# Key-major cross attention on Trainium2: the values product in two runs a turn, and VectorE's row in a new order

## The chip, the cores and the metric

The kernel runs as one program on one core of a Trainium2 chip. The time is that of the device for one execution, in microseconds (us). The span is the time from the first to the last record of the profiled execution. TensorE (PE) multiplies matrices into PSUM, VectorE (DVE) and ScalarE (ACT) work on SBUF and PSUM, GpSimd (POOL) works on SBUF.

## The reference, cut to what matters

The whole model is four layers, each a cross attention and a feed-forward part, over 8 batches of 256 rows of 128 numbers. The change touches only the cross attention of the last layer. There are 16 heads of 64 numbers, and every row attends to 1601 keys and to one learned null key.

```python
scale = DH ** (-0.5)
q = _split_heads(jnp.einsum('bnd,df->bnf', x, Wq))
kv = jnp.einsum('bmc,cf->bmf', context, Wkv)
k, v = jnp.split(kv, 2, axis=-1)
...
k = jnp.concatenate((nk, k), axis=-2)
v = jnp.concatenate((nv, v), axis=-2)
q = q * scale
sim = jnp.einsum('bhid,bhjd->bhij', q, k)
attn = jax.nn.softmax(sim, axis=-1)
out = jnp.einsum('bhij,bhjd->bhid', attn, v)
out = out.transpose(0, 2, 1, 3).reshape(b, -1, INNER)
out = jnp.einsum('bnf,fd->bnd', out, Wout)
```

## The kernel before, in words

`KeyMajorAttention` handles two heads at once. 8 batches times 8 pairs of heads are 64 turns of work, and all products are in float32. Keys lie on the partitions: 13 blocks of 128 keys, and two blocks make a chunk, so that there are 7 chunks (0 to 6; chunk 6 is one block). The work of one turn is spread over three iterations `i` of one loop: in iteration `i` TensorE makes the scores of turn `i` and the keys of turn `i + 1`, softmax and values of turn `i - 1` are worked on, and the values product of turn `i - 2` is made. Each engine has its own loop with this order written out by hand, and they meet through counting semaphores.

- TensorE (`pe_run`) has four groups `g` in an iteration. In each group it makes some of the values product (`pe_meet`, L2282, heads side by side on 64 columns each, the chunks named by `MEETS[g]`), a part of the values (L2217), scores (`pe_score`, L2237, heads side by side on 64 rows each) and a part of the keys (L2207, with the queries L2210 in group 0). In group 0 it transposes the peaks of the scores (L2251) and spreads the shifts (L2258). In group 2 it adds up the exponentials over the partitions (`pe_total`, L2267) ahead of `pe_meet`. `pe_total` waits for all lowered scores, because it writes the PSUM banks from which they are lowered.
- VectorE (`dve_run`) lowers the scores of turn `i - 1` by their peak (`dve_lower`, L2428, four parts for each of the two heads: 8 parts), and raises the running maximum of turn `i` over its chunks (`dve_raise`, L2407, six of them, of which the last is half as large), then `dve_peak` (L2413). It also inverts the total (L2434) and divides the finished values product (`dve_divide`, L2442). The values product of the next turn begins only after `dve_divide` (`out_done`), because it is written over the same PSUM bank.
- ScalarE (`act_run`) copies scores from PSUM (`act_keep`, L2342), takes the exponentials (`act_exp`, L2348, four for the first head after the scores of group 0, four for the second head after those of group 1), and copies values (L2320) and keys (L2325).
- GpSimd (`pool_run`) adds up the exponentials over the chunks (L2493, L2498 and after).
- The projections use two PSUM banks in turn (`due` and `number`); each bank is written again only after it was copied (`taken`). In three turns of a batch (pairs 4, 5 and 6, batches 0 to 6, 21 turns in all) the context of the next batch is transposed as well (L2199): at the places 2, 3 and 4 of the iteration. ScalarE copies those of the places 2 and 4 (L2331), VectorE those of place 3 (L2386, `dve_take_at(dve, i, 3)`). These are called context turns below. In pair 2 of the batches 1 to 7 the output product (L2223) stands at place 3, and VectorE copies it (L2388): seven output turns. 33 of the other full turns (iterations 2 to 62) are called plain.

Of the kernel before, what the change touches and what calls it, by code (L numbers as in the profile page):

```python
# [442 lines left out]
class PairedAttention:  # L443
# [418 lines left out]
    def dve_run(self, dve, out):  # L862
        self.k.nc.vector.memset(self.k.psM[:], 0.0).then_inc(self.partial_zeroed.sem, 1)
        for g in range(-2, self.pairs + 3):
            q, odd = divmod(g, 2)
            for i in range(self.NB):
                for ahead, n in self.score_slots[i]:
                    if 0 <= g + ahead < self.pairs:
                        self.dve_maximum(dve, g + ahead, n)
                        if n == self.steps - 1:  # L870
                            self.dve_shift(dve, g + ahead)
                if i == 2 and odd == 0 and 0 <= q - 2 < self.quads:
                    self.dve_divide(dve, out, q - 2)
# [1197 lines left out]
class KeyMajorAttention:  # L2071
# [13 lines left out]
    CHUNKS = (KB + 1) // 2  # L2085
    NULL = KTAIL + 1
    KEYS = KB * P
    MEETS = [range(0, 2), range(2, 4), range(4, 6), range(6, 7)]

    def __init__(self, k, mem):  # L2090
        self.k = k
# [194 lines left out]
    def pe_run(self, pe):  # L2286
# [4 lines left out]
        for i in range(-1, T + 3):  # L2291
            scores, softmax, meets = 0 <= i < T, 0 <= i - 1 < T, 0 <= i - 2 < T
            for g in range(4):
                if meets and g == 2:
                    self.pe_total(pe, i - 2)
                if meets:
                    for s in self.MEETS[g]:
                        self.pe_meet(pe, i - 2, s)
# [145 lines left out]
    def dve_run(self, dve):  # L2444
        T = self.TURNS
        self.dve_prepare(dve)
        for n in range(0, 8, 2):
            self.dve_take(dve, ("ctx", 0, n))
        for i in range(0, T + 3):
            scores, softmax, meets = 0 <= i < T, 0 <= i - 1 < T, 0 <= i - 2 < T  # L2450
            if softmax:
                self.dve_shift(dve, i - 1)
            self.dve_take_at(dve, i, 0)
            if softmax:
                for part in range(4):
                    self.dve_lower(dve, i - 1, 0, part)
            if scores:
                self.dve_raise(dve, i, 1)
            if softmax:
                self.dve_lower(dve, i - 1, 1, 0)  # L2460
                self.dve_lower(dve, i - 1, 1, 1)
            self.dve_take_at(dve, i, 2)
            if softmax:
                self.dve_lower(dve, i - 1, 1, 2)
                self.dve_lower(dve, i - 1, 1, 3)
            if scores:
                self.dve_raise(dve, i, 2)
                self.dve_raise(dve, i, 3)
            self.dve_take_at(dve, i, 3)
            self.dve_take_at(dve, i, 4)  # L2470
            if meets:
                self.dve_invert(dve, i - 2)
            if scores:
                self.dve_raise(dve, i, 4)
                self.dve_raise(dve, i, 5)
            self.dve_take_at(dve, i, 6)
            if meets:
                self.dve_divide(dve, i - 2)
            if scores:
                self.dve_raise(dve, i, 6)  # L2480
                self.dve_peak(dve, i)
# [836 lines left out]
```

## Time and profile before

| | us |
|---|---|
| median of 3 runs | 4701.62 (4699.08 to 4716.05) |
| the profiled execution's own time | 4698.77 |
| its span | 4697.0 |
| TensorE busy in the span | 3943.0 (84%) |
| VectorE | 3038.2 (65%) |
| ScalarE | 2502.7 (53%) |
| GpSimd | 1560.3 (33%) |

A row of the timeline gives the start of a merged stretch of instructions in us from the start of the span, how long it took, the engine and line, what is written and read, the shape, and how many instructions were merged. PE is a matmul, PEld the load of its weights. A float32 matmul of this kernel has two records. The ends of matmuls are modelled and overlap the next start, so that stretches of TensorE are best measured from start to start. What stands in brackets is the idle time before and who ended it. The last cross attention runs from about 2600 to 4430 us.

### The profile page before, as it was taken

The numbers are of one execution on the slowest core, as the hardware profiler recorded it, in microseconds if no ns is written. First come the engines' busy times: TensorE is split into PE (matmuls) and PEld (weight loads), VectorE is DVE, ScalarE is ACT, GpSimd is POOL, SyncE is SP. The second block draws the span as 40 slices with busy tenths as digits, with TensorE's granted clock in tenths as the row PEclk, the third lists the DMA queues.
The fourth block names the chain that finished last, engine by engine and source line by source line (L and its number), as shares of the span: only waits on it lengthen the run. The fifth ranks groups of instructions, "written<-read, shape, count | busy, mean of one in ns | idle before, by whom it ended". The sixth has DMA issues, their size and how long they took to land. (4 is left out here: it accounts for less than half of the span.)

```text
span 4697.0 us, 74532 instructions
## 1 busy us (share of the span) xinstructions
PE 3943.0 (84%) x28274; PEld 2404.3 (51%) x28274; DVE 3038.2 (65%) x5035; ACT 2502.7 (53%) x4784; POOL 1560.3 (33%) x1285
## 2 busy tenths in 40 slices
PE   2399999899199974888877899999999999999754
PEld 2133333388133333666664566666666666666442
DVE  3399989734277746333333577777777777777757
ACT  2288888733088862333331565556665656666330
POOL 0200000000300001111100477766777776677510
PEclk6599999999589986778878899999999999999877
DMA  5222221100265400000000100000000000000001
GB/s 166 63 48 51 45 47 44 26 16 16 40 88 85 62 2 27 0 0 0 0 8 17 40 15 1 15 1 15 1 15 1 15 1 15 1 1 1 6 17 33
DMA packets 119700, 123.06 MB, mean 26 GB/s; under 512 B 21264, under 2 KB 97648, under 8 KB 118992
## 3 DMA queue, kind: packets, MB, share of 16 engines
q1 hardware_dynamic: 119240, 118.27, 11.7%
q8 instruction: 205, 3.36, 0.3%
q14 instruction: 111, 0.91, 0.1%
q10 hardware_dynamic: 144, 0.52, 0.0%
HBM read 103.02 MB, written 15.73 MB: 25 GB/s over the span
## 5 line engine op out<-in xcount | busy, mean ns | idle before, releaser
L835 DVE TENSOR_REDUCE att_peak.1<-psS 128x1 f32<-128x512 f32 (+1 forms) x1024 | 580.7, 634 | 95.8 <-PE psS L705 95.7
L2498 POOL TENSOR_TENSOR key_sums_0.1<-key_sums_0.1,prob_0.1 128x512 f32<-128x512 f32 x256 | 440.5, 1721 | 28.7 <-POOL key_sums_0.1 L2498 0.4
L2498 POOL TENSOR_TENSOR key_sums_1.1<-key_sums_1.1,prob_1.1 128x512 f32<-128x512 f32 x256 | 421.4, 1646 | 28.4
L804 ACT ACTIVATE att_probT.1<-psT 128x512 f32<-128x512 f32 (+1 forms) x682 | 368.8, 568 | 75.7 <-PE psT L734 34.3
L835 DVE TENSOR_REDUCE att_peak.2<-psS 128x1 f32<-128x512 f32 (+1 forms) x512 | 266.8, 569 | 139.1 <-PE psS L705 137.2
L2407 DVE TENSOR_TENSOR att_highest.1<-att_highest.1,prob_0.1 128x1024 f32<-128x1024 f32 (+1 forms) x160 | 273.1, 1707 | 129.0 <-ACT prob_0.1 L2342 121.6
L2407 DVE TENSOR_TENSOR att_highest.1<-att_highest.1,prob_1.1 128x1024 f32<-128x1024 f32 (+1 forms) x160 | 278.6, 1742 | 115.0 <-ACT prob_1.1 L2342 107.5
L705 PE MATMUL psS<-key_stack.1,query_stack.1 64*128 64x512 bf16 (+1 forms) x1024 | 271.1, 385 | 95.7 <-DMA key_stack.1<-key_parts 48.3
L751 PE MATMUL psM<-att_probT.1,quad_values.1 128*9 128x256 f32 (+1 forms) x3840 | 306.4, 391 | 19.5 <-issue 19.5
L2428 DVE TENSOR_TENSOR prob_0.1<-prob_0.1,psO 128x1024 f32<-128x1024 f32 (+1 forms) x256 | 244.0, 1017 | 49.0 <-PE psO L2258 49.0
L2428 DVE TENSOR_TENSOR prob_1.1<-prob_1.1,psO 128x1024 f32<-128x1024 f32 (+1 forms) x256 | 243.9, 1017 | 49.0 <-PE psO L2258 49.0
L705 PEld LDWEIGHTS psS<-key_stack.1,query_stack.1 64*128 64x128 bf16 x1024 | 78.1, 93 | 355.1 <-issue 194.4
L2493 POOL TENSOR_TENSOR key_sums_0.1<-prob_0.1 128x512 f32<-128x512 f32 x64 | 92.0, 1437 | 494.9 <-ACT prob_0.1 L2348 494.9
L1799 POOL TENSOR_TENSOR head_queries.1<-queryT.1,query_sin.1 64x256 f32<-64x256 f32 x128 | 92.4, 722 | 468.5 <-DVE queryT.1 L1867 460.9
L2342 ACT COPY prob_0.1<-psS 128x1024 f32<-128x1024 f32 (+1 forms) x224 | 203.7, 954 | 72.0 <-PE psS L2237 71.9
L2342 ACT COPY prob_1.1<-psS 128x1024 f32<-128x1024 f32 (+1 forms) x224 | 203.8, 955 | 70.6 <-PE psS L2237 70.6
L807 ACT ACTIVATE att_probT.2<-psT,att_key_bias.1 128x256 f32<-128x256 f32 (+1 forms) x554 | 224.3, 482 | 23.3 <-PE psT L734 18.7
L705 PE MATMUL psS<-key_stack.2,query_stack.2 102*128 102x512 bf16 (+1 forms) x512 | 141.8, 361 | 94.2 <-DMA key_stack.2<-mask_parts 87.4
L2217 PE MATMUL psT<-wkv.1,ctxT_0.1 128*128 128x128 f32 (+1 forms) x1664 | 214.5, 280 | 6.0 <-DVE ctxT_1.1 L2386 5.9
L2217 PE MATMUL psT<-wkv.1,ctxT_1.1 128*128 128x128 f32 (+1 forms) x1664 | 214.9, 280 | 4.5 <-DVE ctxT_0.1 L2386 4.5
L2207 PE MATMUL psM<-ctxT_0.1,wkv.1 128*128 128x512 f32 (+1 forms) x512 | 213.8, 540 | 3.4 <-ACT keyT_0.1 L2325 2.0
L734 PE MATMUL psT<-query_stack.1,key_stack.1 64*128 64x256 bf16 x1279 | 214.9, 282 | 0.5 <-ACT att_probT.1 L804 0.5
(683 smaller groups left out, 8912.3 us busy)
## 6 DMA issues: line engine op xcount, KB each, us to landing
key_stack.1<-key_parts SPq DMA_DIRECT2D x384, 58.0 KB
key_stack.2<-key_parts SPq DMA_DIRECT2D x96, 200.1 KB
ctx_rows.1<-in_ctx_dram SPq DMA_DIRECT2D x8, 1536.0 KB
key_parts<-split_parts.1 SPq DMA_DIRECT2D x8, 1200.8 KB, 5.8
ctx_keys_0.1<-in_ctx_dram SPq DMA_DIRECT2D x4, 768.0 KB
ctx_keys_1.1<-in_ctx_dram SPq DMA_DIRECT2D x4, 768.0 KB
query_stack.1<-query_parts SPq DMA_DIRECT2D x192, 16.0 KB
ctx_values_0.1<-in_ctx_dram SPq DMA_DIRECT2D x4, 768.0 KB
```

The costliest lines, as they stand in the source:

```text
L705: self.k.nc.tensor.matmul(self.score_bank[m % 3][:, 0:w], self.queries(rows, g, h, s * P, P), self.keys(rows, g, h, c0, w), start=True, st ...
L734: last = self.k.nc.tensor.matmul(self.key_bank[(m + h) % 3][0:w, n * S:(n + 1) * S], self.keys(rows, g, h, col, w), self.queries(rows, g, ...
L751: last = self.k.nc.tensor.matmul(self.partial[32 * j:32 * j + self.hd + 1, :], self.vquad[0:w, q % 2, blk, j, :], self.probT[0:w, g % self ...
L804: last = self.k.nc.scalar.activation(probs[:, blks[0]:blks[-1] + 1, :].rearrange("p b q -> p (b q)"), bank[0:w, 0:len(blks) * S], ACT.Exp)
L807: last = self.k.nc.scalar.activation(probs[:, blk, :], bank[0:w, n * S:(n + 1) * S], ACT.Exp, bias=bias)
L835: self.k.nc.vector.tensor_reduce(self.peak[:, 2 * h + s, c:c + 1], self.score_bank[m % 3][:, 0:w], AX_X, ALU.max).then_inc(self.peak_done. ...
L2207: last = nc.tensor.matmul(bank[:, 0:w], self.wkv[:, t, p * P:(p + 1) * P], self.ctxT[b % 2][:, t, n * BANK:n * BANK + w], start=(t == 0), ...
L2217: last = nc.tensor.matmul(bank[0:w, kb % 4 * P:(kb % 4 + 1) * P], self.ctxT[b % 2][:, t, kb * P:kb * P + w], self.wkv[:, t, at:at + P], st ...
L2342: nc.scalar.copy(self.prob[i % 2][:, :, at:at + w], k.psS[:, 2 * (g % 2):2 * (g % 2) + 2, 0:w]).then_inc(self.kept.sem, 1)
L2407: self.k.nc.vector.tensor_tensor(own, old, new, ALU.max).then_inc(self.raised.sem, 1)
L2428: self.k.nc.vector.tensor_tensor(own, own, by, ALU.add).then_inc(self.lowered.sem, 1)
L2498: nc.gpsimd.tensor_tensor(acc, acc, own[:, h, c * BANK:(c + 1) * BANK], ALU.add).then_inc(self.summed.sem, 1)
```

## The change

`MEETS` goes from four pieces of the values product to two: chunks 0 to 3 in group 0 and chunks 4 to 6 in group 2. In groups 1 and 3 `pe_meet` is no longer called. VectorE lowers all eight parts in one row before its first raise, and takes what stands at place 3 directly behind the first raise, ahead of the second and third. The instructions are the same ones in the same number.

```diff
-    MEETS = [range(0, 2), range(2, 4), range(4, 6), range(6, 7)]
+    MEETS = [range(0, 4), (), range(4, 7), ()]
...
             if softmax:
                 for part in range(4):
                     self.dve_lower(dve, i - 1, 0, part)
+            if softmax:
+                for part in range(4):
+                    self.dve_lower(dve, i - 1, 1, part)
+            self.dve_take_at(dve, i, 2)
             if scores:
                 self.dve_raise(dve, i, 1)
-            if softmax:
-                self.dve_lower(dve, i - 1, 1, 0)
-                self.dve_lower(dve, i - 1, 1, 1)
-            self.dve_take_at(dve, i, 2)
-            if softmax:
-                self.dve_lower(dve, i - 1, 1, 2)
-                self.dve_lower(dve, i - 1, 1, 3)
+            self.dve_take_at(dve, i, 3)
             if scores:
                 self.dve_raise(dve, i, 2)
                 self.dve_raise(dve, i, 3)
-            self.dve_take_at(dve, i, 3)
             self.dve_take_at(dve, i, 4)
```

## Rows read from the trace of the kernel before

**Rows 1.** Windows: busy us of each engine in 200 us, then TensorE's granted clock.

```profile
3600.00:3800.00 200.00, 197.75 (x1354) 130.74 (x1353) 155.20 (x133) 123.70 (x178) 143.30 (x101) 1.00 0.03 9
```

**Rows 2.** Timeline, TensorE's stretches in one plain turn.

```profile
3732.09 0.66 PE L2251 MATMUL psO<-tables.1,att_peak.3 128*128 128x128 f32 x4 [0.17 <-DVE att_peak.3 L2413]
...
3737.32 0.65 PE L2210 MATMUL psM<-XT.1,wq.2 128*128 128x256 f32 x2
...
3737.91 1.95 PE L2282 MATMUL psT<-prob_0.1,values_0.1 128*64 128x256 f32 x16
...
3739.78 2.05 PE L2217 MATMUL psT<-wkv.1,ctxT_0.1 128*128 128x128 f32 x16
...
3743.69 1.98 PE L2207 MATMUL psM<-ctxT_1.1,wkv.1 128*128 128x512 f32 x4
...
3745.61 0.65 PE L2267 MATMUL psO<-key_sums_0.1,att_ones.1 128*64 128x256 f32 x4
...
3749.90 2.00 PE L2237 MATMUL psS<-qT_0.1,keyT_0.1 64*128 64x256 f32 x16
...
3753.74 0.65 PE L2282 MATMUL psT<-prob_0.1,values_0.1 66*64 66x256 f32 x4
...
3754.32 0.65 PE L2217 MATMUL psT<-wkv.1,ctxT_0.1 128*65 128x128 f32 x4
...
3757.45 1.95 PE L2282 MATMUL psT<-prob_1.1,values_1.1 128*64 128x256 f32 x16
...
3759.59 0.66 PE L2251 MATMUL psO<-tables.1,att_peak.3 128*128 128x128 f32 x4 [0.19 <-DVE att_peak.3 L2413]
```

**Rows 3.** Timeline, TensorE in iteration 1, which has no values product.

```profile
2635.36 0.65 PE L2210 MATMUL psM<-XT.1,wq.2 128*128 128x256 f32 x2
2635.85 1.95 PE L2217 MATMUL psT<-wkv.1,ctxT_0.1 128*128 128x128 f32 x16
2637.73 0.49 PE L2237 MATMUL psS<-qT_1.1,keyT_1.1 64*128 64x256 f32 x2
```

**Rows 4.** Waits: who waited for whom, us in total, times, longest.

```profile
PE psT L2217 <- DVE ctxT_1.1 L2386: 5.9, 12, 0.8
...
PE psT L2217 <- DVE ctxT_0.1 L2386: 4.5, 9, 0.8
```

**Rows 5.** Timeline, VectorE and ScalarE in the plain turn of Rows 2.

```profile
3735.01 3.81 DVE L2428 TENSOR_TENSOR prob_1.1<-prob_1.1,psO 128x1024 f32<-128x1024 f32 x4 [1.53 <-PE psO L2258]
...
3738.40 3.25 ACT L2348 ACTIVATE prob_1.1<-prob_1.1 128x1024 f32<-128x1024 f32 x4
...
3739.88 3.81 DVE L2428 TENSOR_TENSOR prob_1.1<-prob_1.1,psO 128x1024 f32<-128x1024 f32 x4
...
3747.35 1.75 DVE L2434 RECIPROCAL att_rtotal.4<-psO 128x256 f32<-128x256 f32 x1
...
3752.12 1.83 DVE L2407 TENSOR_TENSOR att_highest.1<-att_highest.1,prob_0.1 128x1024 f32<-128x1024 f32 x1 [3.03 <-ACT prob_0.1 L2342]
...
3756.09 0.41 DVE L2442 TENSOR_TENSOR att_outT.3<-psT,att_rtotal.4 128x256 f32<-128x256 f32 x1
...
3757.88 1.65 DVE L2413 TENSOR_TENSOR att_peak.3<-att_highest.1 128x512 f32<-128x512 f32 x1
```

**Rows 6.** Instructions of lines 2407 and 2428: duration in ns, least/median/greatest, first and last start.

```profile
L2407 DVE TENSOR_TENSOR att_highest.1<-att_highest.1,prob_1.1 x160: 956/1844/2327, 2642.5 to 4404.4; 128x1024 f32<-128x1024 f32 x128, 128x512 f32<-128x512 f32 x32
L2407 DVE TENSOR_TENSOR att_highest.1<-prob_0.1 x32: 1218/1220/1226, 2619.7 to 4360.9; 128x1024 f32<-128x1024 f32 x32
...
L2428 DVE TENSOR_TENSOR prob_1.1<-prob_1.1,psO x256: 414/1216/1222, 2658.8 to 4417.6; 128x1024 f32<-128x1024 f32 x128
```

**Rows 7.** Timeline, a context turn: transposed context of place 2, the copies by ScalarE.

```profile
3628.05 0.60 PE L2199 MATMUL psM<-tables.1,ctx_rows.1 128*128 128x128 f32 x4
3628.24 0.59 ACT L2320 COPY values_1.1<-psT 128x512 f32<-128x512 f32 x1 [0.22 <-PE psT L2217]
...
3628.57 2.00 PE L2237 MATMUL psS<-qT_0.1,keyT_0.1 64*128 64x256 f32 x16
3628.73 0.59 ACT L2331 COPY ctxT_1.1<-psM 128x512 f32<-128x512 f32 x1
```

## The prediction

> **What bounds the kernel now.** I read the 40 slices of the page first, to find the stage of the change, then the windows over it, then the waits in it, and last the timeline of single turns. The windows show what sets the time of this stage: TensorE is busy for 197.75 of 200 us, at a granted clock of 1.00 (its upper level, 2.4 GHz), while VectorE has 155, GpSimd 143 and ScalarE 124 [rows 1]. So a turn takes as long as TensorE's row of it, plus the few waits of TensorE that are left. In the timeline a plain turn runs from one transpose of peaks to the next, 3732.09 to 3759.59, 27.50 us [rows 2]. I call its start W and count from there. "Busy" doesn't mean that every stretch is at its shortest: the gain of this change, if any, lies inside the busy time, in what a change of kind costs, and in two small waits.
>
> The waits. The values product of chunks 0 and 1 takes 1.87 us from start to next start (3737.91 to 3739.78 is such a piece), yet at the turn's end the transposes come 2.14 us after its start (3757.45 to 3759.59): TensorE waits about 0.26 us for VectorE's peak [rows 2]. In the context turns it waits before the third piece of values until VectorE has copied the transposed context: 10.4 us in 21 waits [rows 4].
>
> **Part 1, two pieces less.** What a piece costs beyond its matmuls is read by setting a turn with it beside one without it. With it: queries 0.59 (3737.32 to 3737.91), product 1.87, values and scores 3.91 (3739.78 to 3743.69) [rows 2]. Without it: queries 0.49 (2635.36 to 2635.85) and values 1.88 up to the scores [rows 3]. Scores take 1.92 (scores and keys together 3.84, 3749.90 to 3753.74, and keys 1.92, 3743.69 to 3745.61 [rows 2]), which leaves 1.99 for values behind a product. So values are 0.10 shorter where no product precedes them, and queries 0.10. The matmuls of the product themselves: 16 records last 1.95, 4 records last 0.65, so a pair of heads costs (1.95 - 0.65) / 6 = 0.217 us, eight pairs 1.73 [rows 2]. Joined to another run, the second piece costs 1.73 in place of 1.87. Removed as a piece of its own it gives back 0.10 + 0.14 + 0.10 = 0.34 us in group 1.
>
> In group 3 the piece is chunk 6 alone: 0.58 (3753.74 to 3754.32), of which two pairs are 0.43, so 0.15; the keys ahead of it get 0.09 shorter as the queries did; for the short values behind it (65 columns) the entry is not shown by itself: at least nothing, at most the 0.10 above, and I take 0.05. That is 0.29. Together 0.63 us a turn (0.58 to 0.68), in 61 full turns (iterations 2 to 62): 38.4 us.
>
> **Part 2, TensorE's new row.** W; group 0 up to the queries' end 5.82 - 0.09 = 5.73; values and scores 3.91 - 0.10, so keys at 9.54; total at 11.46 (keys 1.92); total, product, values were 4.29 (3745.61 to 3749.90) and get the two pairs of chunk 6, 0.43, so the scores of chunks 4 and 5 start at S = 16.18; with the next keys 3.84 - 0.09, short values at 19.93; these, the last scores and keys 3.13 - 0.05, so the product of chunks 0 to 3 starts at 23.01; it takes 1.87 + 1.73, and the transposes could start at 26.61 [rows 2]. Now every waiting point of that row, against the engine that it waits for:
> - Peaks: VectorE's peak ends 3757.88 + 1.65 - 3749.90 = 9.63 after S in the old turn [rows 2, 5]; with S = 16.18 that is 25.8, 0.8 before TensorE. The wait of 0.26 goes, in 33 plain turns: 8.6 us.
> - The product of the next turn waits for the division, which ends 3756.09 + 0.41 - 3749.90 = 6.60 after S, at 22.8; TensorE comes at 23.0. Hidden by only 0.2.
> - The total waits for the last lowering. The first row of lowering starts at W + 2.92 and ends at 6.7; the second follows directly now and takes 3.81, so it ends at 10.5 [rows 5]; TensorE comes at 11.46. Hidden by 0.9.
> - VectorE must be free at S + 2.22 = 18.4 for raise 4, as before (3752.12 - 3749.90) [rows 2, 5]. From 10.5 it has raises 1, 2, 3 and the inversion of 1.75. Raises 2 and 3 with their wait took 3747.35 - 3743.69 = 3.66; the first took 1.22 while it stood before GpSimd's sums [rows 6], and now it falls among them. A raise costs up to 2.33 there. With 2.1 for it: 10.5 + 2.1 + 3.7 + 1.75 = 18.05. Just free, 0.35 to spare.
>
> The Trainium skill has a rule that speaks against this move of the first raise: the page GPSIMD Engine Reference, section Specifications, says that GpSimd shares its SBUF interfaces with VectorE and contends with VectorE instructions that have two SBUF inputs. The trace agrees on raises, 1.22 us ahead of the sums and up to 2.33 beside them; by the rule alone the first raise would take 0.9 us more, and a turn would lose up to that if VectorE's row decided it.
>
> **Part 3, context turns.** The copy of place 3 moves before raises 2 and 3. The context is ready at about 13.1, VectorE has by then raised once (at most 12.6), copies, and TensorE needs the bank only at 15.8. The waits of 10.4 us go; from start to start they are some 0.05 longer each, 11.5 us. The price lies behind the copy: raises 2 and 3 wait for it, then end at 13.8 + 2 x 2.1 = 18.0, the inversion at 19.8, and raise 4 is due at 20.2. Hidden.
>
> But something else comes early. In group 1 TensorE reaches the keys sooner, by the product that left (1.87 + 0.19), and these keys need the bank of the context of place 2, which ScalarE copies only after its four exponentials. Those end at 3738.40 + 3.25 - 3732.09 = W + 9.56 [rows 5], then come the copy of values and that of context, 0.49 apart and 0.59 long [rows 7]: done at 10.6. TensorE is there at 9.54 + 0.52 for the transposes (3628.05 to 3628.57) less the 0.09 that values save before them = 9.97 [rows 7]. A new wait of 0.65 us, 21 times: 13.7 us lost. In the plain turn the same keys wait only for the copy of group 0, long done.
>
> Output turns: the output is made at W + 15.1 and copied at 15.6, raises 2 and 3 end at 19.8, the inversion at 21.5, raise 4 is due at 22.0. Hidden by 0.5. The ends: in iteration 63, with no keys, TensorE waits for lowering, which ends 1.1 us sooner: about 0.9 gained. The first turns and the drain behind the last are unchanged, at 0 within 1 us each.
>
> **Sum.** 38.4 + 8.6 + 11.5 + 0.9 - 13.7 = 45.7, less about 0.7 for small waits on the division in the seven turns of pair 6. 45 us. The profiled execution took 4698.77 (span 4697.0), so it would take 4653.8. The median of the runs shown lies 2.9 above the profiled one; I forecast 4655.
>
> **Rivals.**
> 1. VectorE becomes the bound. Slacks of 0.2 and 0.35 us are small, and GpSimd's sums fall differently on the raises. If raises 4 and 5 took 2.33 each in place of 3.97 for both, the division would end 0.7 later, and every turn would wait 0.5: 61 x 0.5 = 30 us, 4684. If all raises take 2.33, the peak ends at 10.5 + 5 x 2.33 + 1.75 + 1.79 (division to peak) + 1.65 = 27.4 and plain turns gain 0.1 only; then 4680 to 4690. For it: the median raise is at 1.84 and VectorE has little air. Against: raises 4 and 5 together took 3.97 in the same company. 12%.
> 2. A piece costs nothing by itself; what I read as its price would be in the neighbours anyway. Then only waits change: -8.6 - 11.5 + 13.7 = -6, 4693 to 4697, no change. Against: turns with and without the piece differ cleanly [rows 2, 3]. 5%.
> 3. Slower: the second row of lowering, now wholly in one piece ahead of the raises, is slowed as raises are, 2.1 in place of 1.13 a part. It would end at 13.7, the total would wait 2.2 us, the plain turn would be 28.8, 1.3 above before, and 33 of them give +44: 4740. It decides from the point at which lowering ends later than 11.46 + 0.9 = W + 12.4. Against: half of these parts ran beside GpSimd already, and the longest of 256 took 1.222, the median 1.216 [rows 6]. 2%.
> 4. No new wait in context turns: 14 us more gain, 4641. It is within the range, 10%.
>
> The same page of the Trainium skill bears on rival 3: lowering has one input in PSUM and one in SBUF, which its rule doesn't name as contending; the trace agrees, 1.222 us at most.
>
> **How the numbers follow.** My forecast has 71% (its own range 4647 to 4670, from 0.58 or 0.68 a turn, 3 us each way, the new wait between 0.3 and 1.0, 7 us, and up to 0.15 on the division), rival 4 has 10, rival 1 has 12, rival 2 has 5, rival 3 has 2. A measurement of this kernel tells a change from none at about 0.5%, 23.5 us: faster is below 4678. The forecast, rival 4 and a quarter of rival 1 are faster: 0.84; the rest of rival 1 and rival 2 are the same: 0.14; slower is rival 3, 0.02. The range of 8 in 10 runs from rival 4 to the middle of rival 1: 4639 to 4679.
>
> **What the profile would show.** Plain turns of 26.6 us from transpose to transpose; queries 0.49 before values; runs of 32 and 20 records on L2282; no wait of L2251 for VectorE; no wait of L2217 for L2386; 21 waits of L2207 for ScalarE's L2331, 0.65 each. It would be wrong if L2282 waits for L2442 in plain turns, if raises 1 to 3 run past W + 18.4, or if the step within a long run of the product is above 0.217.

## The result, and the profile after

| | before | after |
|---|---|---|
| median of 6 runs, us | 4702.64 (4695.24 to 4716.05) | 4668.53 (4663.09 to 4681.94) |
| ratio | | 0.9928, 95% interval 0.9908 to 0.9948 |
| span of the profiled execution, us | 4697.0 | 4670.1 |

The changed kernel is faster by 34 us (24 to 43 by the interval), that is 0.72%. The forecast was 4655, 48 us below this median of before; the range of 4639 to 4679 holds the time. The direction and the terms of the gain were right, but a quarter of the forecast gain is missing, and one of the prediction's own signs of being wrong came true: the product waits for the division in plain turns.

Windows of the changed kernel: the same stretch as in [rows 1].

```profile
3600.00:3800.00 200.00, 197.51 (x1403) 137.47 (x1400) 166.08 (x133) 118.06 (x173) 147.31 (x103) 1.00 0.03 9
```

TensorE is as busy as before, but it does 1403 records in the time in which it did 1354, and VectorE went from 155 to 166 us of 200. The timeline of one plain turn of the changed kernel, TensorE's stretches, against [rows 2] and [rows 3]:

```profile
2852.12 0.66 PE L2251 MATMUL psO<-tables.1,att_peak.3 128*128 128x128 f32 x4
...
2857.36 0.65 PE L2210 MATMUL psM<-XT.1,wq.2 128*128 128x256 f32 x2
...
2857.84 1.95 PE L2217 MATMUL psT<-wkv.1,ctxT_1.1 128*128 128x128 f32 x16
...
2859.72 2.00 PE L2237 MATMUL psS<-qT_1.1,keyT_1.1 64*128 64x256 f32 x16
...
2863.57 0.65 PE L2267 MATMUL psO<-key_sums_1.1,att_ones.1 128*64 128x256 f32 x4
2864.05 2.33 PE L2282 MATMUL psT<-prob_1.1,values_1.1 128*64 128x256 f32 x20
2866.31 2.05 PE L2217 MATMUL psT<-wkv.1,ctxT_1.1 128*128 128x128 f32 x16
2868.29 2.00 PE L2237 MATMUL psS<-qT_1.1,keyT_1.1 64*128 64x256 f32 x16
...
2875.42 3.67 PE L2282 MATMUL psT<-prob_0.1,values_0.1 128*64 128x256 f32 x32 [0.24 <-DVE att_outT.3 L2442]
...
2879.02 0.66 PE L2251 MATMUL psO<-tables.1,att_peak.3 128*128 128x128 f32 x4
```

The turn takes 26.90 us from transpose to transpose, against 27.50. Queries take 0.48 and values 1.88, as they did in the turn without a product. W is again the start of the transposes, here 2852.12. The scores of chunks 4 and 5 start at W + 16.17 (forecast: 16.18). The last transposes wait for nothing any more. But the product of 32 records now waits for VectorE's division: it starts at W + 23.30 where the forecast had 23.01.

VectorE in the same turn, against [rows 5]:

```profile
2855.04 7.54 DVE L2428 TENSOR_TENSOR prob_0.1<-prob_0.1,psO 128x1024 f32<-128x1024 f32 x8 [1.53 <-PE psO L2258]
...
2862.50 2.19 DVE L2407 TENSOR_TENSOR att_highest.1<-prob_1.1 128x1024 f32<-128x1024 f32 x1
...
2864.80 4.33 DVE L2407 TENSOR_TENSOR att_highest.1<-att_highest.1,prob_1.1 128x1024 f32<-128x1024 f32 x2
...
2869.06 1.74 DVE L2434 RECIPROCAL att_rtotal.4<-psO 128x256 f32<-128x256 f32 x1
...
2870.72 4.31 DVE L2407 TENSOR_TENSOR att_highest.1<-att_highest.1,prob_1.1 128x1024 f32<-128x1024 f32 x2
...
2874.96 0.41 DVE L2442 TENSOR_TENSOR att_outT.3<-psT,att_rtotal.4 128x256 f32<-128x256 f32 x1
...
2876.75 1.64 DVE L2413 TENSOR_TENSOR att_peak.3<-att_highest.1 128x512 f32<-128x512 f32 x1
```

The eight parts of lowering end at W + 10.46, as forecast, and none takes longer beside GpSimd. The five large raises take 2.1 to 2.2 us each. Raise 4 begins when VectorE comes free, at W + 18.60, not when its scores are there. From W + 2.92 to the end of the division at W + 23.25 VectorE has no idle time. So in plain turns one chain runs through both engines and closes: transposes, shifts, all of VectorE's row up to the division, the product of 32 records, the next transposes. That chain, and not TensorE's row alone, sets the 26.90 us, although TensorE is busy for 197.51 of 200 us.

The waits of the changed kernel's TensorE in iterations 2 to 62 (who waited for whom, us in total, times, longest), against [rows 4]:

```profile
PE psT L2282 <- DVE att_outT.3 L2442: 7.9, 32, 0.3
...
PE psM L2207 <- ACT ctxT_1.1 L2331: 6.6, 12, 0.6
...
PE psM L2207 <- ACT ctxT_0.1 L2331: 4.9, 9, 0.6
```

The 21 waits for VectorE's copy of the context are gone, and 21 new ones for ScalarE's copy stand there, as the forecast had it. The first row is the one that it had at nearly nothing: it put 0.7 us for the seven turns of pair 6. Those seven don't wait; the 33 plain turns and the seven second context turns (pair 5) do.

How to compare kernels finely: before this stage the executions differ by themselves. The transposes of iteration 2 start at 2655.86 in the profile of before and at 2659.95 after, and between 2648 and 2663 in the profiles of the experiments, and nearly all of it stands ahead of anything that an edit touches: the transposes of iteration 1 already start at 2630.13 and 2634.66. What the edits touch ahead of iteration 2 is iteration 1 itself (25.73 us before, 25.29 in the changed kernel, 24.12 with the order alone). From there to the transposes of iteration 63 every turn of one kind takes the same time within some 0.03 us (one exception stands below the table). I call this stretch of 61 turns "the 61 turns": 1725.9 us before (2655.86 to 4381.74), 1691.0 after (2659.95 to 4350.96), 34.9 less. Each value is of one execution, but each kind of turn stands in it seven or 33 times. The intervals of the ratios overlap between several of the kernels with the two pieces, so it is these turns that tell those kernels apart.

### The profile page after: what moved, and what is told of

Read it like the earlier page. It is cut to its first block and busy times, and to the rows that moved or that the text cites. A ratio compares the mean times of both kernels' runs of the same rounds, so it can differ in the third digit from the quotient of the medians.

```text
span 4670.1 us, 74527 instructions
## 1 busy us (share of the span) xinstructions
PE 3915.6 (84%) x28269; PEld 2435.1 (52%) x28274; DVE 3150.6 (67%) x5035; ACT 2479.5 (53%) x4784; POOL 1585.6 (34%) x1285
## 5 line engine op out<-in xcount | busy, mean ns | idle before, releaser
L2495 POOL TENSOR_TENSOR key_sums_0.1<-key_sums_0.1,prob_0.1 128x512 f32<-128x512 f32 x256 | 448.0, 1750 | 28.7 <-POOL key_sums_0.1 L2495 0.4
L2495 POOL TENSOR_TENSOR key_sums_1.1<-key_sums_1.1,prob_1.1 128x512 f32<-128x512 f32 x256 | 435.6, 1702 | 28.4
L2407 DVE TENSOR_TENSOR att_highest.1<-att_highest.1,prob_1.1 128x1024 f32<-128x1024 f32 (+1 forms) x160 | 309.5, 1934 | 20.2 <-ACT prob_1.1 L2342 10.1
L2407 DVE TENSOR_TENSOR att_highest.1<-att_highest.1,prob_0.1 128x1024 f32<-128x1024 f32 (+1 forms) x160 | 285.1, 1782 | 38.9 <-ACT prob_0.1 L2342 30.5
L2490 POOL TENSOR_TENSOR key_sums_0.1<-prob_0.1 128x512 f32<-128x512 f32 x64 | 82.1, 1282 | 461.7 <-ACT prob_0.1 L2348 461.7
L2207 PE MATMUL psM<-ctxT_0.1,wkv.1 128*128 128x512 f32 (+1 forms) x512 | 211.5, 535 | 10.0 <-ACT ctxT_1.1 L2331 6.6
L2207 PE MATMUL psM<-ctxT_1.1,wkv.1 128*128 128x512 f32 (+1 forms) x512 | 211.5, 536 | 4.9 <-ACT ctxT_0.1 L2331 4.9
L2237 PE MATMUL psS<-qT_0.1,keyT_0.1 64*128 64x256 f32 x1664 | 214.3, 392 | 0.7 <-ACT keyT_0.1 L2325 0.7
```

The lines of the kernel that those rows point to most:

```text
L2207: last = nc.tensor.matmul(bank[:, 0:w], self.wkv[:, t, p * P:(p + 1) * P], self.ctxT[b % 2][:, t, n * BANK:n * BANK + w], start=(t == 0), ...
L2237: last = nc.tensor.matmul(k.psS[:, 2 * (g % 2) + h, blk % 2 * S:(blk % 2 + 1) * S], self.keyT[i % 2][own, blk * P:(blk + 1) * P], self.qT[ ...
L2407: self.k.nc.vector.tensor_tensor(own, old, new, ALU.max).then_inc(self.raised.sem, 1)
L2495: nc.gpsimd.tensor_tensor(acc, acc, own[:, h, c * BANK:(c + 1) * BANK], ALU.add).then_inc(self.summed.sem, 1)
```

## The experiments

In each, the turns are measured from transpose to transpose; "context turns" are those of pairs 4, 5 and 6 in this order.

| kernel | ratio to before (95%) | 61 turns | plain turn | context turns | output turn |
|---|---|---|---|---|---|
| before | | 1725.9 | 27.50 | 29.01, 29.01, 28.11 | 30.81 |
| changed | 0.9928 (0.9908 to 0.9948) | 1691.0 | 26.91 | 28.52, 28.33, 27.70 | 30.16 |
| pieces alone | 0.9939 (0.9926 to 0.9953) | 1693.6 | 26.89 | 28.59, 28.59, 27.82 | 30.16 |
| order alone | 0.9991 (0.9978 to 1.0003) | 1723.3 | 27.73 | 28.73, 28.17, 27.75 | 30.81 |
| pieces and early copy | one run | 1689.8 | 26.89 | 28.51, 28.14, 27.80 | 30.16 |
| early division | 0.9905 (0.9886 to 0.9924) | 1679.2 | 26.59 | 28.51, 28.14, 27.70 | 30.16 |
| early copies by ScalarE | 0.9887 (0.9870 to 0.9903) | 1676.7 | 26.91 | 27.90, 27.53, 27.09 | 30.16 |
| both of these | 0.9884 (0.9867 to 0.9900) | 1666.3 | 26.59 | 27.90, 27.52, 27.09 | 30.16 |
| short sums | one run | 1679.2 | 26.59 | 28.51, 28.14, 27.70 | 30.16 |
| three pieces, early division | one run | 1733.0 | 27.73 | 29.47, 28.54, 28.53 | 30.46 |
| three pieces, late division | 0.9938 (0.9913 to 0.9962) | 1697.8 | 26.90 | 28.81, 28.44, 28.00 | 30.46 |

With three pieces and the early division two of the seven first context turns take 28.9, the others 29.47.

### The two pieces alone

```diff
-    MEETS = [range(0, 2), range(2, 4), range(4, 6), range(6, 7)]
+    MEETS = [range(0, 4), (), range(4, 7), ()]
```

Expected: 

> The product in two pieces alone, VectorE's order as before. Theory (a piece costs 0.34 and 0.29 us by itself): queries take 0.49 and values behind them 1.88 again, chunks 0 to 3 take 3.60, the wait for the peak goes. The total comes at W + 11.46 and lowering ends at 11.6, so 0.2 us of wait there; plain turns 26.8 (33 x 0.7 = 23 us less). In context turns the copy by VectorE still stands behind raises 2 and 3, and TensorE comes sooner: a wait of 0.6 on ScalarE and 0.8 to 1.1 on VectorE, these turns gain nothing. Together 20 to 28 us less than before, ratio 0.994 to 0.996. Rival (a piece costs nothing, only waits changed): plain turns 27.3 to 27.5, ratio 0.998 to 1.002.

Measured: 28.7 us less by the ratio (0.9939, just beyond the expected 20 to 28), 32.3 less in the 61 turns. Its waits:

```profile
PE psM L2207 <- ACT ctxT_1.1 L2331: 6.5, 12, 0.6
...
PE psO L2267 <- DVE prob_0.1 L2428: 5.3, 23, 0.2
...
PE psO L2267 <- DVE prob_1.1 L2428: 2.3, 10, 0.2
...
PE psT L2217 <- DVE ctxT_1.1 L2386: 1.5, 4, 0.4
...
PE psT L2217 <- DVE ctxT_0.1 L2386: 1.1, 3, 0.4
```

Plain turns are 26.89, where 26.8 was expected: the total waits 0.30 from start to start (0.2 as recorded) for the last lowering. Context turns gained 0.4, 0.4 and 0.3, where I had expected nothing. VectorE's copy of the context came sooner than I had worked out, at 15.0 us into the turn in place of 16.4 before, and only seven turns show a recorded wait for it. The rival, that a piece costs nothing, is out: with it plain turns could not be below 27.3.

### The new order alone

The diff is that of the change without its first hunk.

Expected: 

> VectorE's new order alone, the product in four pieces. Theory: the 21 waits on VectorE's copy of the context go (11.5 us less), and all raises fall among GpSimd's sums at 2.1 to 2.2 us each, so that the peak of plain turns comes up to 0.25 later than before (0 to 8 us more): 3 to 11 us less, ratio 0.9975 to 0.9995; no wait on ScalarE's copy of the context. Rival (the order is what gave the gain): 20 us less or more.

Measured: no difference that can be told (0.9991), 2.6 us less in the 61 turns. The waits on the copy are gone, and the context turns are 10.4 us shorter together; plain turns are 0.24 longer, 8 us: their transposes now wait 0.50 for the peak in place of 0.26. The order trades one against the other, near the lower end of what the theory had.

### The pieces, and only the early copy

```diff
     (against the pieces alone)
                 self.dve_lower(dve, i - 1, 1, 3)
+            self.dve_take_at(dve, i, 3)
             if scores:
                 self.dve_raise(dve, i, 2)
                 self.dve_raise(dve, i, 3)
-            self.dve_take_at(dve, i, 3)
```

Expected: 

> The two pieces with VectorE's old rows of lowering and raise 1 between them, but the copy of place 3 ahead of raise 2. Theory (of VectorE's new order only the early copy is worth anything, 2.6 us): waits on VectorE's copy go, plain turns 26.89 with the wait of 0.3 before the total, context turns 0.1 to 0.4 shorter than with the pieces alone; iterations 2 to 62 within 2 us of the changed kernel's 1691, or below it. Rival (lowering in one row is needed): 1694 or more.

Measured: 1689.8, within 2 us of the changed kernel and on the better side (the context turns are shorter than with the pieces alone by 0.08, 0.45 and 0.01, where 0.1 to 0.4 was expected). So the moved copy is what the new order brings, 3.9 us beside the pieces. Lowering in one row brings nothing: it takes away the 0.30 that the total waits for lowering, and puts the 0.31 that the product waits for the division in its place.

### The division directly behind the inversion

```diff
             if meets:
                 self.dve_invert(dve, i - 2)
+                self.dve_divide(dve, i - 2)
...
-            if meets:
-                self.dve_divide(dve, i - 2)
```

Expected: 

> The changed kernel, with the division directly behind the inversion, ahead of raise 4. Theory (the 0.31 us that plain turns wait before the product is for the division, which is late because it stands behind two raises of 2.1 us): the product waits no more, the peak comes 0.3 us before TensorE needs it, plain turns 26.6; 33 x 0.31 and 7 x 0.19, 11.5 us less than the changed kernel, and in iteration 63 the idle 4 us before the product and its half clock go, 3 us more. The profiled span is 4655, the ratio to before 0.989 to 0.991. Rival (VectorE's row as a whole is the bound): the wait only moves to the peak, plain turns stay at 26.9.

Measured: plain turns 26.59, the second context turn 28.14, and the 61 turns 11.8 us shorter than in the changed kernel. The wait for the division is gone and none for the peak came:

```profile
PE psM L2207 <- ACT ctxT_1.1 L2331: 6.5, 12, 0.5
...
PE psM L2207 <- ACT ctxT_0.1 L2331: 4.9, 9, 0.5
```

The theory holds; the rival would have left plain turns at 26.9. The span was expected at 4655 and is 4662.3. Iteration 2 of this profiled execution started 3.0 us later than in the changed kernel's. Iteration 63 is 3.3 shorter, as expected (25.83 in place of 29.16), but from its end to the end of the span it is 294.3 us in place of 290.0. Of these 4.3 us 1.5 stand in the first 16 records of the values of iteration 64: they took 3.24 us in place of 1.79, since the granted clock was 0.50 from 4369 to 4372. Where the rest lies was not followed up.

### ScalarE's copies between its exponentials

```diff
             for g in range(4):
-                self.act_take_at(act, i, 2 * g)
+                if g != 1 or not softmax:
+                    self.act_take_at(act, i, 2 * g)
...
                     for part in range(4):
+                        if g == 0 and part == 2:
+                            self.act_take_at(act, i, 2)
                         self.act_exp(act, i - 1, g, part)
```

Expected: 

> The changed kernel, with ScalarE copying what stands at place 2 (values, context) behind the second of its four exponentials of the first head, not behind the fourth. Theory (the new wait of 0.6 us before the keys of group 1 in context turns is for ScalarE's copy): those 21 waits go, 8 to 13 us less than the changed kernel, context turns 0.4 to 0.6 shorter, plain turns unchanged at 26.9. Rival (the late half of the exponentials delays kept scores, raises or GpSimd's sums): a new wait of the same size elsewhere, context turns as before or plain turns longer.

Measured: 14.3 us less than the changed kernel in the 61 turns, a little more than expected. Context turns are 0.62, 0.80 and 0.61 shorter, plain turns the same. The second context turn also lost its wait for the division. This is the cause of the 21 waits: what TensorE waits for in the changed kernel is a copy queued behind exponentials that nobody needs at once. Its timeline in a context turn of the changed kernel:

```profile
3609.47 3.26 ACT L2348 ACTIVATE prob_1.1<-prob_1.1 128x1024 f32<-128x1024 f32 x4
...
3612.62 0.58 ACT L2320 COPY values_1.1<-psT 128x512 f32<-128x512 f32 x1
...
3613.08 0.60 ACT L2331 COPY ctxT_1.1<-psM 128x512 f32<-128x512 f32 x1
...
3613.74 1.98 PE L2207 MATMUL psM<-ctxT_0.1,wkv.1 128*128 128x512 f32 x4 [0.54 <-ACT ctxT_1.1 L2331]
```

### Both together

The two diffs above.

Expected: 

> Both edits on the changed kernel: the division behind the inversion, and ScalarE's copies behind its second exponential. Theory (the two waits are independent): plain turns 26.6, context turns 27.9, 27.5 and 27.1, output turns 30.16, iterations 2 to 62 together 1666 us against 1691 in the changed kernel; ratio to before 0.984 to 0.988. Rival (once both are gone VectorE's row decides, by its 0.3 us of air): plain or context turns are 0.2 or more longer than these.

Measured: 1666.3 in the 61 turns, as added up; 4642.92 us median (4641.42 to 4649.91), ratio 0.9884, which is 0.0004 above the expected span of ratios. It has the lowest time of this study, 24.7 us below the changed kernel in the 61 turns. By the ratios it can't be told from the early copies alone (0.9887); the turns tell them apart, 10.4 us in the 61. Its windows, in the stretch of [rows 1], show no idle time of TensorE at all:

```profile
3600.00:3800.00 200.00, 200.00 (x1401) 138.03 (x1401) 170.79 (x135) 121.71 (x179) 149.35 (x103) 1.00 0.03 9
```

### Short sums on GpSimd

```diff
-            nc.gpsimd.tensor_tensor(acc, acc, own[:, h, c * BANK:(c + 1) * BANK], ALU.add)
+            nc.gpsimd.tensor_tensor(acc[:, 0:8], acc[:, 0:8], own[:, h, c * BANK:c * BANK + 8], ALU.add)
```

Expected: 

> The changed kernel, in which GpSimd's middle sums (8 of 14 per turn, L2498) work on 8 columns in place of 512, so that the totals leave out most keys. Theory (raises 1 to 5 take 2.1 us in place of 1.22 because GpSimd works beside them, and that is what makes the division late): raises that stand clear of the remaining sums take 1.22, the wait before the product goes, plain turns 26.6. Rival (raises take 2.1 because of what stands before them on VectorE, or for their own operands): they stay at 2.1 and plain turns at 26.9.

Measured: plain turns 26.59 and no wait for the division, with VectorE's order untouched. The instructions of line 2407 in this kernel (ns least/median/greatest), and below them those of lines 2407 and 2428 in the changed one:

```profile
L2407 DVE TENSOR_TENSOR att_highest.1<-att_highest.1,prob_0.1 x160: 691/1225/2129, 2623.0 to 4331.1; 128x1024 f32<-128x1024 f32 x128, 128x512 f32<-128x512 f32 x32
...
L2407 DVE TENSOR_TENSOR att_highest.1<-prob_0.1 x32: 1224/1546/1558, 2620.9 to 4319.6; 128x1024 f32<-128x1024 f32 x32
```

```profile
L2407 DVE TENSOR_TENSOR att_highest.1<-att_highest.1,prob_0.1 x160: 693/1934/2122, 2626.4 to 4347.2; 128x1024 f32<-128x1024 f32 x128, 128x512 f32<-128x512 f32 x32
...
L2407 DVE TENSOR_TENSOR att_highest.1<-prob_0.1 x32: 1226/2204/2215, 2624.3 to 4334.4; 128x1024 f32<-128x1024 f32 x32
...
L2428 DVE TENSOR_TENSOR prob_0.1<-prob_0.1,psO x256: 409/1211/1222, 2637.6 to 4361.0; 128x1024 f32<-128x1024 f32 x128
```

The median raise falls from 1.93 to 1.23 us, and raise 1 from 2.20 to 1.55. Only GpSimd's work was cut, so it is what makes the raises slow, and the slow raises are what made the division late. Lowering stays at 1.21 beside the sums, in the changed kernel too.

### Three pieces, with the early division

```diff
     (against the early division)
-    MEETS = [range(0, 4), (), range(4, 7), ()]
+    MEETS = [range(0, 4), (), range(4, 6), range(6, 7)]
```

Expected: 

> The kernel with the early division (plain turns 26.59, no waits), with chunk 6 back in group 3 as a piece of its own. Theory (a piece costs by itself): 0.29 us a turn more, plain turns 26.88: 0.15 in the product, 0.09 in the keys ahead, 0.05 in the values behind. Rival (a piece costs nothing where TensorE does not wait): 26.59.

Measured: neither. Plain turns are 27.73, longer than before the change. VectorE in one of them:

```profile
2847.01 1.74 DVE L2434 RECIPROCAL att_rtotal.4<-psO 128x256 f32<-128x256 f32 x1
...
2850.41 0.42 DVE L2442 TENSOR_TENSOR att_outT.3<-psT,att_rtotal.4 128x256 f32<-128x256 f32 x1 [1.66 <-PE psT L2282]
...
2850.75 5.32 DVE L2407 TENSOR_TENSOR att_highest.1<-att_highest.1,prob_0.1 128x1024 f32<-128x1024 f32 x3
...
2857.81 0.66 PE L2251 MATMUL psO<-tables.1,att_peak.3 128*128 128x128 f32 x4 [0.78 <-DVE att_peak.3 L2413]
```

The division needs the whole product, and chunk 6 is now made in group 3. So the division held VectorE up for 1.66 us, with raises 4 to 6 and the peak queued behind it, and TensorE then waited 0.8 for the peak. I had changed two things at once. What the run does show, set beside the next one (1697.8): with chunk 6 in group 3 the early division costs 35 us in the 61 turns, where with two pieces it gained 11.8. It pays only because the product ends in group 2, that is, because of the two pieces.

### Three pieces, with the late division

The same edit against the changed kernel.

Expected: 

> The changed kernel with chunk 6 back in group 3 as a piece of its own; the division where the changed kernel has it, so that nothing on VectorE waits for chunk 6 early. Theory (a piece costs 0.29 us by itself, and TensorE waits for the division only because it now comes early): plain turns 26.59 + 0.29 = 26.88, with no wait before the product, since TensorE comes 0.7 us later after the scores of chunks 4 and 5; context turns 0.29 longer than in the changed kernel where they had no such wait, output turns 30.45; iterations 2 to 62 about 5 to 9 us more than 1691. Rival (a piece costs nothing): plain turns 26.6, about 1681.

Measured: 1697.8, 6.7 more than the changed kernel. Turns that wait for no division grew by 0.29 to 0.30: context turns 28.52 to 28.81 and 27.70 to 28.00, output turns 30.16 to 30.46. In plain turns the piece costs what the wait had cost, 26.90:

```profile
2704.03 0.65 PE L2282 MATMUL psT<-prob_1.1,values_1.1 66*64 66x256 f32 x4
2704.61 0.65 PE L2217 MATMUL psT<-wkv.1,ctxT_0.1 128*65 128x128 f32 x4
2705.19 0.70 PE L2237 MATMUL psS<-qT_1.1,keyT_1.1 64*128 64x256 f32 x4
```

The theory's 0.29 is right, and so is that TensorE only waits for the division if it comes early. In the changed kernel the second removed piece therefore gave nothing in the 33 plain turns.

## Why the prediction was right, and where it was off

- **What bounds the kernel**: right for the kernel before, where VectorE still stood idle for 3.03 us of a plain turn [rows 5], and for output turns and most context turns. In plain turns of the changed kernel it no longer held: VectorE's row up to the division has no idle time and paces the turn, which is what rival 1 said, in a milder form. With the division moved ahead of raises 4 and 5 and the copies early, TensorE's row alone sets the time again, 200.00 of 200 us busy.
- **Part 1, the price of a piece**: right. 0.63 a turn was forecast. The plain turn without any wait is 26.59 (early division, short sums); 27.50 less its wait of 0.26 is 27.24, so it is 0.65, or 39.7 us in 61 turns where 38.4 was forecast. The 0.29 for the piece of chunk 6 has a run of its own (three pieces, late division). The rest is read from rows: queries went from 0.59 to 0.48, the values behind them from 1.99 to 1.88, two runs of 1.87 became one of 3.60. What in the change from one kind of matmul to the other costs this time (the 64 columns, the weights, the PSUM bank) no run separates. The short values behind chunk 6, taken as 0.05, went from 0.58 to 0.53. Of rival 2 nothing is left.
- **Part 2, the peak**: right, the wait is gone, 8.6 us. The margin was forecast as 0.8; the peak ended 0.63 ahead of the transposes, and 0.3 of that is there only because TensorE had waited for the division. Lowering ended where forecast, and rival 3 is out.
- **Part 2, the division**: this is the step that failed, in its size. "Hidden by only 0.2" became a wait of 0.31 in 33 plain turns and of 0.19 in 7 context turns. By the early division that is 11.8 us, where 0.7 was in the sum, and 0.15 a turn at most in the forecast's own range. The cause is the estimate for raises 1 to 3: I took 2.1 and, for raises 2 and 3, the old 3.66, and had VectorE free at W + 18.05. From start to next start they took 2.30 and 4.26, and VectorE was free only at 18.60, after raise 4 had been due at 18.40. Raises 4 and 5 then took 4.24 in place of 3.97 up to the division, which ended at W + 23.25 in place of 22.8. So rival 1 came true in part, 12 of its 30 us. The upper bound of 2.33 a raise was in the text; the value that I took was too near the old mean, although the change pushes all raises among the sums.
- **The rule on shared interfaces** from the Trainium skill (GPSIMD Engine Reference, Specifications) spoke against moving raise 1. The trace agrees: raise 1 went from 1.22 to 2.20, 0.98 more where 0.9 was worked out for it, lowering stayed at 1.21, and with short sums the median raise is back at 1.23. I should have given it a larger part in the sum.
- **Part 3, context turns**: right. The 21 waits on VectorE are gone. The new 21 waits on ScalarE were forecast at 0.65 and are 0.61 from start to start: 12.9 us where 13.7 was forecast. Rival 4 is out.
- **The forecast's own number**: the sum gives 4653.8 for the profiled execution and 2.9 more for the median, 4656.7; the 4655 that was written is 1.7 below that.
- **The ends**: wrong. Iteration 63 was to gain 0.9 and lost 3.4 (25.80 to 29.16). Timeline of the kernel before there, and timeline and windows of the changed kernel:

```profile
4404.53 1.95 PE L2282 MATMUL psT<-prob_0.1,values_0.1 128*64 128x256 f32 x16 [2.96 <-DVE att_outT.3 L2442]
4407.54 0.66 PE L2251 MATMUL psO<-tables.1,att_peak.3 128*128 128x128 f32 x4 [1.06 <-DVE att_peak.3 L2413]
```

```profile
4368.79 0.70 PE L2237 MATMUL psS<-qT_1.1,keyT_1.1 64*128 64x256 f32 x4
4373.75 6.44 PE L2282 MATMUL psT<-prob_0.1,values_0.1 128*64 128x256 f32 x32 [4.26 <-DVE att_outT.3 L2442]
4380.12 0.66 PE L2251 MATMUL psO<-tables.1,att_peak.3 128*128 128x128 f32 x4
```

```profile
4370.00:4372.00 2.00, 0.00 (x0) 0.00 (x0) 1.90 (x2) 0.13 (x1) 1.86 (x2) 1.00 0.00 0
4374.00:4378.00 4.00, 4.00 (x20) 2.17 (x20) 2.67 (x2) 0.00 (x0) 3.63 (x4) 0.50 0.00 0
```

  With no keys to make, TensorE reached the product early and stood idle for 4.3 us waiting for the division. The granted clock was still 1.00 from 4370 to 4372 and 0.50, the lower level, from 4374 to 4378. The product of 32 records took 6.37 us in place of 3.60, so 2.8 of the 3.4 us stand in it. With 3.60 the turn would have been 26.4, still 0.6 longer than before: behind the division there now stand four chunks of the product ahead of the transposes, where there were two. The prediction looked at the wait for lowering alone and left out this one. No run holds the clock up by itself; with the early division the turn took 25.83.

Added up: 39.7 + 8.6 + 11.5 - 12.9 - 11.8 = 35.1, and the 61 turns are 34.9 us shorter. With iteration 63, which is 3.4 longer, and iteration 1, which is 0.4 shorter, that is 31.9; the rest of the difference in the medians, 34, is within its interval.

## What to carry to other kernels

When TensorE is "99% busy", look at what a change from one kind of matmul to another costs, by a stretch that lacks the neighbour: here 0.29 to 0.34 us for each piece of the product set between other work, and joining them gave more (39.7 us) than the removed waits together (20.1). A share of 99% doesn't say that the engine sets the pace either: follow one turn from a point back to the same point, through every engine that stands in between. When a faster bounding engine comes sooner to all its meeting points, list each with its margin, and price the other engine's row by its durations in the new company, not by the old mean; a margin of 0.2 us on work of 2 us is no margin. A short copy or division that frees a buffer belongs directly behind what it needs, ahead of long work that nobody waits for, but only where what it needs is surely done.

## What the runs showed of the hardware

- A raise (VectorE, 128x1024 float32, both inputs in SBUF) takes 1.22 us alone and 2.1 to 2.2 in a row beside GpSimd's additions (128x512), which take from 1.26 to 2.20 us themselves in the changed kernel. VectorE's lowering of the same size with one input in PSUM takes 1.21 in either case.
- Within the product, the cost of a pair of heads was the same in short and long runs: from start to next start 4 records (two pairs) took 0.58 us, 16 took 1.87 and 32 took 3.60, that is 0.215 and 0.216 a pair. Entering and leaving took the same whether the run was short or long: 0.58 - 2 x 0.216 = 0.15 with 4 records, 3.60 - 16 x 0.216 = 0.14 with 32. The run of 20, which stands directly behind the total of the same 128x64 form, took 2.26, or 0.10 beside its ten pairs.
- In iteration 63 of the changed kernel TensorE was idle for 4.26 us, and the granted clock was 0.50 for most of the product behind it; the transposes behind that product took 0.49 us again, as in every other turn.
